# Graph network: every sixth group gathers three tiles, ScalarE copies the columns of the fourth

## The chip, the cores and the metric

The kernel runs on one core of a Trainium2 chip. The metric is the device time of one execution in microseconds; the time before is the median of three runs.

## The reference

Two message-passing layers over 6250 nodes with 128 features and 200,000 edges, which are sorted by destination. In each layer every edge takes a row of its source, a row of its destination and its own 128 features:

```python
# layer 0
m = relu(concat([x[dst], x[src], edge_attr, u[0]]) @ W1.T + b1)
x = layernorm(x + relu(concat([x, segment_sum(m, dst), u[0]]) @ W2.T + b2))
# layer 1
h = relu(concat([x[src], x[dst], edge_attr]) @ msg_w1 + msg_b1)
agg = segment_sum(h @ msg_w2 + msg_b2, dst) / counts
x = layernorm(x + relu(concat([x, agg]) @ upd_w1 + upd_b1) @ upd_w2 + upd_b2)
```

The product with the concatenation is a sum of three products, so what an edge needs of its source is one row of q = x @ wq (128 fp32 numbers), and of its destination one row of p = x @ wp + b.

## The kernel before

**Tiles.** Edges go in groups of 512 = 4 tiles (J = 4) of 128 (P); there are NG = 391 groups in a layer, numbered i = l * NG + g over both. The tables of q (tabQ, one for each layer) and p (tabP, three bf16 pieces to a row) lie in DRAM.

**One group.** GpSimd gathers the q rows of its edges into the ring Q, which holds R_Q = 10 groups: one indirect DMA a tile (L319), by the list of sources srcE in SBUF. The gather of group i waits until VectorE's addition of group i - 10 is done. TensorE multiplies the transposed edge features by wc into a PSUM bank (L1119, fp32) and adds the p rows with a one-hot matrix ST that VectorE makes (L1302, L1124). VectorE adds bank and Q into M (L1405), ScalarE applies the relu to M in place (L1287), and TensorE sums the edges of a destination with a second one-hot matrix S (L1392, L1137), two groups later in its order. VectorE adds these sums to AC (L1429) at a column that it reads from a register; registers come from baseI in SBUF (L960). ScalarE waits for the addition of each group before its relu, and TensorE for the relu.

**What runs beside it.** In layer 0, groups 2 to 40, the rest of tabP is made, a chunk every three groups (rows_product, rows_hi, rows_mid, rows_store). When all edges of a block of nodes ("unit" u, 14 of them) are summed, its update follows in steps that are spread over groups by the tables DUE and STEPS: first and second (normalisation), norm, x1t (transposition), xt_copy (to XT), q1, q_copy (store to tabQ and, for the early units, tabE), hi, mid, p_store. XT holds the transposed x: of layer 0 until a unit's update, of layer 1 from then on. Layer 1 gathers its first three groups (EARLY, 12 gathers) from tabE and then waits for the whole of tabQ. Each engine runs its own program in order; where an engine waits, all that stands behind it on that engine waits too. Before all this, 20 gathers fetch raw rows of x (L325), which are multiplied by wq on the chip.

Of the kernel before, what the change touches and what calls it, by code (L numbers as in the profile page):

```python
# [8 lines left out]
I32 = mybir.dt.int32  # L9
# [5 lines left out]
N = 6250  # L15
# [85 lines left out]


# [19 lines left out]
def build(nc, a, out):  # L122
    ctx = ExitStack()
    with ctx:
# [44 lines left out]
        srcR = sb("srcR", [P, RAW * J], I32)  # L169
        vsum = sb("vsum", [P, 1])  # L170
# [59 lines left out]
        p1 = {n: sem(f"p1_{n}") for n in ("c", "hi", "r", "mid", "lo")}  # L230
        s_mz, s_mean, s_ind, s_u, s_ru, s_meet = (sem(n) for n in ("s_mz", "s_mean", "s_ind", "s_u", "s_ru", "s_meet"))
# [76 lines left out]

        def q_count(i):
            return 16 * sum(tiles(x % NG) for x in range(i % R_Q, i + 1, R_Q))  # L310
# [96 lines left out]
        def start_scalar(e):  # L407
            e.dma_start(wall[:, 0:D], a["wall"][:, 0:D]).then_inc(s_wq, 16)
            for i in range(1, len(XG), 2):
                x_load(e, i)  # L410
            e.dma_start(wall[:, NLATE:NW], a["wall"][:, NLATE:NW]).then_inc(s_wl, 16)
            e.dma_start(rows3[:, :, :].rearrange("p a d -> p (a d)"), a["rows"].broadcast_to([3, 4 * D])).then_inc(s_row, 16)
            e.dma_start(baseI[:, :], a["base"]).then_inc(s_bas, 16)
            e.dma_start(basE, a["base"].broadcast_to([P, NGP])).then_inc(s_bas, 16)
            e.dma_start(cb[:, :], a["rows"][:, 3 * D:4 * D].broadcast_to([P, D])).then_inc(s_cb, 16)
            for c in range(1, NC, 2):
                n = CH[c][1]
                e.wait_ge(s_q, c + 1)
# [40 lines left out]
        def start_vector(e):  # L459
# [7 lines left out]
            def bases_to_rows():  # L467
                e.wait_ge(s_bas, 32)
# [152 lines left out]
        def general_gpsimd(e, l):  # L621
            q = gs[l]
            e.wait_ge(q["z"], 16)
            if l == 0:
                for r in range(PF):
                    e.wait_ge(f_q[r], 16 * J)
# [380 lines left out]
        def fast_tensor(e):  # L1007
# [31 lines left out]
            def q1(u):  # L1039
# [4 lines left out]
                for k in range(n):  # L1044
                    last = e.matmul(bank[o][:, k * D:(k + 1) * D], XT[:, (b + k) * P:(b + k + 1) * P], wq[1], start=(k == 0), stop=(k == n - 1))  # L1045
# [4 lines left out]
                for k in range(n):  # L1050
                    last = e.matmul(bank[3][:, k * D:(k + 1) * D], XT[:, (b + k) * P:(b + k + 1) * P], wp[1], start=False, stop=(k == n - 1))  # L1051
# [6 lines left out]
            def hidden(u):  # L1058
# [47 lines left out]
            for l in range(2):  # L1106
                for g in range(LAST + 6):
                    i = l * NG + g
                    if g < NG:
# [51 lines left out]
        def fast_scalar(e):  # L1161
# [90 lines left out]

            for l in range(2):
                for g in range(LAST + 11):
                    if l == 0:
# [27 lines left out]
                    if g < NG:  # L1283
                        i = l * NG + g
                        e.wait_ge(v_tt, i + 1)
                        m = M[:, i % R_M, 0:tiles(g), :].rearrange("p j d -> p (j d)")
                        e.activation(m, m, ACT.Relu).then_inc(v_rl, 1)  # L1287

        def fast_vector(e):
# [49 lines left out]
            def second(l, u):  # L1339
# [5 lines left out]
                if l == 0:  # L1345
                    e.memset(AC[:, 0, b * P:(b + n) * P], 0.0).then_inc(s_mz, 1)
# [30 lines left out]
            for l in range(2):  # L1377
                ctl = 2 - l
                for g in range(LAST + 10):
# [13 lines left out]
                    if 1 <= g < NG + 1:  # L1393
# [10 lines left out]
                        n = tiles(g - 1)  # L1404
# [12 lines left out]
                    if 3 <= g < NG + 3 and last_of(l * NG + g - 3):  # L1417
# [8 lines left out]
                        if w == NWIN:  # L1426
# [3 lines left out]
                                        ALU.add).then_inc(v_ag, 1)  # L1430
                    if l == 0:
# [131 lines left out]
def laid_out(v):  # L1563
    import numpy as _np

    def cut(m, b):
# [18 lines left out]
        "srcL": srcp.astype(_np.int32).reshape(NGP, J, P).transpose(2, 0, 1).reshape(P, NGP * J),  # L1585
        "dstL": dstp.astype(_np.int32).reshape(NGP, J, P).transpose(2, 0, 1).reshape(P, NGP * J),
# [23 lines left out]
```

## Time and profile before

| | us |
|---|---|
| runs, median (lowest to highest) | 3929.21 (3928.15 to 3929.58) |
| profiled execution, its span | 3929.8 |
| GpSimd busy | 2960.2 |
| TensorE matmul busy, weight loads busy | 3229.0, 2975.7 |
| VectorE busy | 1583.8 |
| ScalarE busy | 590.4 |

The profile is of one execution; beside its span it gives no other time of it. Busy time is that of the instructions an engine executes. Instructions that only its sequencer handles (registers, semaphores, issuing a DMA) are not counted. "Issue" is idle time in which the engine waited for nothing that the profile shows. PE stands for TensorE's matmuls, PEld for its weight loads, DVE for VectorE, ACT for ScalarE, POOL for GpSimd, SP for SyncE; a q behind a name is its sequencer. PEclk is the granted share of TensorE's full speed, 2.4 GHz.

### The profile page before, as it was taken

The numbers are of one execution on the slowest core, as the hardware profiler recorded it, in microseconds if no ns is written. First come the engines' busy times: TensorE is split into PE (matmuls) and PEld (weight loads), VectorE is DVE, ScalarE is ACT, GpSimd is POOL, SyncE is SP. The second block draws the span as 40 slices with busy tenths as digits, with TensorE's granted clock in tenths as the row PEclk, the third lists the DMA queues.
The fourth block names the chain that finished last, engine by engine and source line by source line (L and its number), as shares of the span: only waits on it lengthen the run. The fifth ranks groups of instructions, "written<-read, shape, count | busy, mean of one in ns | idle before, by whom it ended". The sixth has DMA issues, their size and how long they took to land.

```text
span 3929.8 us, 45222 instructions
## 1 busy us (share of the span) xinstructions
PE 3229.0 (82%) x16881; PEld 2975.7 (76%) x16881; DVE 1583.8 (40%) x3640; ACT 590.4 (15%) x1017; POOL 2960.2 (75%) x3156
## 2 busy tenths in 40 slices
PE   6988888888788888888878888878888888888887
PEld 6877777777777777777778777777777777777776
DVE  6533334343444444444543333333433333333333
ACT  1211111111111111111111111111111111111111
POOL 7777777777777777777777777777777777777776
PEclk7755555565655556665665555555555555555556
DMA  7644444444444444445454444444444444444443
GB/s 261 200 138 134 135 136 143 132 133 139 148 139 149 149 149 147 147 147 154 131 158 135 133 131 124 135 139 136 139 136 141 139 142 137 140 135 141 142 142 100
DMA packets 257760, 563.18 MB, mean 143 GB/s; under 512 B 131254, under 2 KB 151713, under 8 KB 232572
## 3 DMA queue, kind: packets, MB, share of 16 engines
q1 hardware_dynamic: 132824, 332.20, 25.4%
q0 software_dynamic: 100032, 205.00, 19.8%
q10 hardware_dynamic: 24676, 23.01, 1.7%
q8 instruction: 135, 2.21, 0.2%
q14 instruction: 93, 0.76, 0.1%
HBM read 537.29 MB, written 22.66 MB: 142 GB/s over the span
## 4 chain that ended last, share of the span: by engine, by line
POOL 70%; issue 23%; DMA 4%; DVE 2%; PE 2%; ACT 0%; SPq 0%; POOLq 0%; DVEq 0%
POOL Qr L319 70%; DMA Qr<-tabQ,srcE 3%; DVE BIG L1405 1%; PE bank L1137 0%; DMA srcE<-in_srcL 0%; DVE BIG L1302 0%; PE bank L1119 0%; PE bank L1092 0%; DVE BIG L1392 0%; DMA tabQ<-BIG 0%; DVE BIG L1400 0%; PE bank L1051 0%; PE bank L1045 0%; DVE AC L609 0%; POOL Qr L325 0%
## 5 line engine op out<-in xcount | busy, mean ns | idle before, releaser
L319 POOL DMA_INDIRECT Qr<-tabQ,srcE x3094 | 2925.3, 945 | 942.9 <-issue 933.2
L1137 PE MATMUL bank<-BIG 128*128 128x42 f32 x6252 | 1379.0, 396 | 143.6 <-ACT BIG L1287 141.1
L1119 PE MATMUL bank<-wall,BIG 128*128 128x128 f32 x6252 | 1473.0, 410 | 19.1 <-DMA BIG<-tabP 19.1
L1137 PEld LDWEIGHTS bank<-BIG 128*128 128x128 f32 x6252 | 1307.5, 308 | 207.6 <-ACT BIG L1287 201.5
L1302 DVE TENSOR_TENSOR BIG<-bank,BIG 126x512 bf16<-126x512 f32 x782 | 539.3, 690 | 2264.7 <-DMA Qr<-tabQ,srcE 2254.8
L1119 PEld LDWEIGHTS bank<-wall,BIG 128*128 128x128 f32 x6252 | 1311.5, 309 | 23.8 <-issue 23.8
L1287 ACT ACTIVATE BIG<-BIG 128x512 f32<-128x512 f32 (+1 forms) x782 | 492.1, 629 | 3229.1 <-DVE BIG L1405 3220.4
L1124 PE MATMUL bank<-BIG 126*128 126x128 bf16 x3126 | 490.2, 295 | 506.5 <-DVE BIG L1302 396.7
L1124 PEld LDWEIGHTS bank<-BIG 126*128 126x128 bf16 x3126 | 342.0, 135 | 639.0 <-DVE BIG L1302 455.9
L1405 DVE TENSOR_TENSOR BIG<-bank,Qr 128x512 f32<-128x512 f32 (+1 forms) x782 | 532.7, 681 | 41.2 <-PE bank L1124 25.3
L1392 DVE TENSOR_TENSOR BIG<-bank,relE 128x168 f32<-128x168 f32 x782 | 252.6, 323 | 3.5 <-DMA Qr<-tabQ,srcE 3.5
L1400 DVE TENSOR_REDUCE BIG<-BIG 128x42 bf16<-128x168 f32 (+2 forms) x263 | 151.7, 577 | 0.0
L1429 DVE TENSOR_TENSOR AC<-AC,bank 128x84 f32 (+1 forms) x526 | 111.1, 211 | 6.7 <-PE bank L1137 3.2
L1140 PEld LDWEIGHTS bank<-BIG,onesb 128*128 128x128 bf16 x263 | 70.4, 268 | 0.0
L1140 PE MATMUL bank<-BIG,onesb 128*128 128x42 bf16 x263 | 60.5, 230 | 0.0
L609 DVE RECIPROCAL AC<-AC 128x512 f32<-128x512 f32 (+1 forms) x13 | 41.1, 3159 | 0.0
L1013 PE MATMUL bank<-wall,XT 128*128 128x128 f32 x98 | 26.1, 444 | 0.0
L1013 PEld LDWEIGHTS bank<-wall,XT 128*128 128x128 f32 x98 | 21.9, 326 | 5.4 <-issue 5.2
L1056 PE MATMUL bank<-XT,wall 128*128 128x512 f32 (+2 forms) x28 | 25.4, 1019 | 0.0
L325 POOL DMA_INDIRECT Qr<-in_x,srcR x20 | 20.6, 1031 | 6.0 <-issue 5.7
L1045 PE MATMUL bank<-wall,XT 128*128 128x128 f32 x98 | 23.1, 404 | 0.9 <-ACT XT L1180 0.9
L1026 PE MATMUL bank<-wall,AC 128*128 128x128 f32 x98 | 23.0, 410 | 0.4 <-DVE AC L1429 0.4
(137 smaller groups left out, 609.9 us busy)
## 6 DMA issues: line engine op xcount, KB each, us to landing
BIG<-in_eaT SPq DMA_DIRECT2D x194, 1024.0 KB, 5.4
BIG<-in_dstR SPq DMA_DIRECT2D x194, 504.0 KB
Qr<-tabQ,srcE POOLq DMA_INDIRECT x3094
BIG<-tabP SPq DMA_DIRECT2D x526, 31.5 KB
tabP<-BIG ACTq DMA_DIRECT2D x22, 384.0 KB, 3.1
tabQ<-BIG ACTq DMA_DIRECT2D x17, 256.0 KB, 5.2
X<-in_xN SPq DMA_DIRECT2D x1, 3136.0 KB, 16.8
tabE<-BIG ACTq DMA_DIRECT2D x11, 256.0 KB, 2.3
```

Of the source, the lines that this page charges most:

```text
L319: e.indirect_dma_start(Q[0:p, i % R_Q, j, :], None, table[:, :], bass.IndirectOffsetOnAxis(ap=srcE[0:p, g, j:j + 1], axis=0)).then_inc(f_q ...
L1013: e.matmul(bank[o][:, k * D:(k + 1) * D], XT[:, (b + k) * P:(b + k + 1) * P], w2T[0], start=False, stop=False)
L1119: e.matmul(bank[i % R_C][:, j * D:(j + 1) * D], f_eaT[:, k % R_EA, (g % LQ * J + j) * P:(g % LQ * J + j + 1) * P], wc[l], start=(j == 0), ...
L1124: last = e.matmul(bank[i % R_C][:, j * D:(j + 1) * D], ST[0:K, i % R_ST, j * P:(j + 1) * P], PB[0:K, w % R_PB, :], start=False, stop=(j == ...
L1137: last = e.matmul(sums[:, 0:W], M[:, i % R_M, j, :], S[:, hot(i), j, :], start=(j == 0 and first_of(i)), stop=(j == n - 1 and last_of(i)))
L1140: last = e.matmul(sums[:, W:2 * W], onesb[:, :], S16[:, w % R_S, :], start=True, stop=True)
L1287: e.activation(m, m, ACT.Relu).then_inc(v_rl, 1)
L1302: e.tensor_tensor(ST[0:K, i % R_ST, :], bank[6][0:K, g:g + 1].broadcast_to([K, GE]), bc[0:K, k % R_BC, (g % LQ) * GE:(g % LQ + 1) * GE], A ...
L1392: e.tensor_tensor(S[:, hot(i), :, :], io, rel, ALU.is_equal).then_inc(v_s, 1)
L1400: e.tensor_reduce(S16[:, w % R_S, :], S[:, h:hot(i) + 1, :, :].rearrange("p r j w -> p w (r j)"), AX, ALU.add).then_inc(v_cn, 1)
L1405: e.tensor_tensor(M[:, i % R_M, 0:n, :].rearrange("p j d -> p (j d)"), bank[i % R_C][:, 0:n * D], Q[:, i % R_Q, 0:n, :].rearrange("p j d - ...
L1429: e.tensor_tensor(acc, acc, bank[4 + w % 2][:, 0:ctl * W].rearrange("p (t w) -> p t w", w=W), ALU.add).then_inc(v_ag, 1)
```

## The change

In groups 10, 16, 22, ... to 388 of layer 0 and from 16 on in layer 1, GpSimd gathers three tiles. The fourth tile's part of q is not gathered: ScalarE copies the columns of XT that belong to the tile's 128 sources into a tile XC (ring of two), and TensorE multiplies that by wq straight into the group's bank. The 128 columns are copied in six parts of 20, 20, 24, 20, 20 and 24, one behind each group's relu, in the six groups 6n to 6n + 5 for the tile of group 6n + 10. Each part loads its column numbers from colI (SBUF) into registers; each copy takes one column, 128 partitions by one element. VectorE adds only three tiles in such a group, and ScalarE takes the relu of the fourth from the bank. As XT must keep the x of layer 0 until the last such tile, xt_copy writes layer 1's x to AC, which is free by then; q1 reads it there; and xt_move copies it to XT at the end of layer 0, from group 384 on, the last three units in group 0 of layer 1, behind which VectorE clears AC.

```diff
+MOVES = [(0, NG - 7 + u // 2) for u in range(NU - 3)] + [(1, 0)] * 3
+MOVED = 2
+COPIERS = ((6, 10),)
+TAKEN = [[[n * per + lead for n in range(NG) if n * per + lead < NG - 2 and n * per >= (0, MOVED)[l]] for l in range(2)]
+         for per, lead in COPIERS]
...
+def col_piece(k, l, g):
+    per, lead = COPIERS[k]
+    n, q = divmod(g, per)
+    if n * per + lead not in TAKEN[k][l]:
+        return None
+    return col_tile(l * NG + n * per + lead)[1], COL_ROW[k] + n, 4 * (q * P // 4 // per), 4 * ((q + 1) * P // 4 // per), q == 0
...
+        def gathered(i):
+            return tiles(i % NG) - (col_tile(i) is not None)
...
-                for j in range(tiles(g)):
+                for j in range(gathered(i)):
                     p = VP if g == NG - 1 and j == VJ else P
                     e.indirect_dma_start(Q[0:p, i % R_Q, j, :], None, table[:, :],
...
-                    last = e.matmul(bank[o][:, k * D:(k + 1) * D], XT[:, (b + k) * P:(b + k + 1) * P], wq[1], start=(k == 0), stop=(k == n - 1))
+                    last = e.matmul(bank[o][:, k * D:(k + 1) * D], AC[:, 0, (b + k) * P:(b + k + 1) * P], wq[1], start=(k == 0), stop=(k == n - 1))
...
+                        if col_tile(i) is not None:
+                            h, c = col_tile(i)
+                            e.wait_ge(s_col[h], COPIERS[h][0] * (c + 1))
+                            e.matmul(bank[i % R_C][:, (J - 1) * D:J * D], XC[h][:, c % R_X, :], wq[l], start=False, stop=False)
...
-                e.copy(XT[:, b * P:(b + n) * P], bank[unit_bank(0, "x1t", u)][:, 0:n * P]).then_inc(u_tc, 1)
+                e.copy(AC[:, 0, b * P:(b + n) * P], bank[unit_bank(0, "x1t", u)][:, 0:n * P]).then_inc(u_tc, 1)
+
+            def xt_move(u):
+                b, n = UN[u]
+                e.wait_ge(u_tc, u + 1)
+                if u == 0:
+                    for k, (per, _) in enumerate(COPIERS):
+                        e.wait_ge(s_col[k], per * len(TAKEN[k][0]))
+                e.copy(XT[:, b * P:(b + n) * P], AC[:, 0, b * P:(b + n) * P]).then_inc(s_mv, 1)
...
+            def columns(l, g):
+                if col_piece(0, l, g) is None:
+                    return
+                c, row, lo, hi, new = col_piece(0, l, g)
+                if new and c >= R_X:
+                    e.wait_ge(v_C, col_group(0, c - R_X) + 1)
+                if new and c == len(TAKEN[0][0]):
+                    e.wait_ge(s_mv, NU)
+                _, at = nc.values_load_multi_w_load_instructions(
+                    colI[row:row + 1, lo:hi], engines=[mybir.EngineType.Activation], min_val=0, max_val=N - 1,
+                    skip_runtime_bounds_check_because="the source of an edge, which is a node")
+                for x in range(lo, hi):
+                    last = e.copy(XC[0][:, c % R_X, x:x + 1], XT[:, bass.ds(at[x - lo], 1)])
+                last.then_inc(s_col[0], 1)
...
-                        m = M[:, i % R_M, 0:tiles(g), :].rearrange("p j d -> p (j d)")
-                        e.activation(m, m, ACT.Relu).then_inc(v_rl, 1)
+                        m = M[:, i % R_M, 0:gathered(i), :].rearrange("p j d -> p (j d)")
+                        last = e.activation(m, m, ACT.Relu)
+                        if col_tile(i) is not None:
+                            last = e.activation(M[:, i % R_M, J - 1, :], bank[i % R_C][:, (J - 1) * D:J * D], ACT.Relu)
+                        last.then_inc(v_rl, 1)
+                        columns(l, g)
...
-                if l == 0:
-                    e.memset(AC[:, 0, b * P:(b + n) * P], 0.0).then_inc(s_mz, 1)
+
+            def clear(u):
+                b, n = UN[u]
+                e.wait_ge(s_mv, u + 1)
+                e.memset(AC[:, 0, b * P:(b + n) * P], 0.0).then_inc(s_mz, 1)
```

The order of the instructions shows it in three places. GpSimd's whole list of gathers, before:

```order
L325 DMA Qr<-in_x,srcR 128x128 x20
L319 DMA Qr<-tabQ,srcE 128x128 x20
L1454 TENSOR_LOAD flagI
L1454 ISA x2
L1491 COMPARE_AND_BRANCH
L319 DMA Qr<-tabQ,srcE 128x128 x1522
L319 DMA Qr<-tabQ,srcE 64x128
L319 DMA Qr<-tabE,srcE 128x128 x12
L319 DMA Qr<-tabQ,srcE 128x128 x1550
L319 DMA Qr<-tabQ,srcE 64x128
```

and now:

```order
L361 DMA Qr<-in_x,srcR 128x128 x20
L355 DMA Qr<-tabQ,srcE 128x128 x20
L1533 TENSOR_LOAD flagI
L1533 ISA x2
L1570 COMPARE_AND_BRANCH
L355 DMA Qr<-tabQ,srcE 128x128 x1458
L355 DMA Qr<-tabQ,srcE 64x128
L355 DMA Qr<-tabE,srcE 128x128 x12
L355 DMA Qr<-tabQ,srcE 128x128 x1487
L355 DMA Qr<-tabQ,srcE 64x128
```

Of the two long runs on tabQ, 64 gathers left the first and 63 the second; all else stands as it stood.

ScalarE around group 10 of layer 0, before (L1287 is the relu of a group, L1251 the store of a chunk of tabP, L1243 and L1247 its two copies):

```order
L1243 CAST BIG<-bank 128x4x128
L1287 ACTIVATE BIG<-BIG 128x512
L1251 DMA tabP<-BIG 128x4x384
L1287 ACTIVATE BIG<-BIG 128x512
L1247 CAST BIG<-bank 128x4x128
L1287 ACTIVATE BIG<-BIG 128x512
```

and now, in group 10 (L1356 and L1358 are the relus, L1312 the register load, L1316 the pairs of a register instruction, ISA, and a copy of one column):

```order
L1302 DMA tabP<-BIG 128x4x384
L1356 ACTIVATE BIG<-BIG 128x384
L1358 ACTIVATE BIG<-bank 128x128
L1312 TENSOR_LOAD colI
L1316 ISA
L1316 COPY XC<-XT 128x1
L1316 ISA
```

The relu has become two, and a load and 20 or 24 pairs stand between it and the next group's relu; before there was nothing between most relus.

TensorE around group 10, before (L1119 the edge features, L1124 the p rows, L1137 the sums, L1140 the counts):

```order
L1119 MATMUL bank<-wall,BIG 128x128 x4
L1124 MATMUL bank<-BIG 128x128 x4
L1137 MATMUL bank<-BIG 128x42 x4
L1140 MATMUL bank<-BIG,onesb 128x42
L1119 MATMUL bank<-wall,BIG 128x128 x4
L1124 MATMUL bank<-BIG 128x128 x4
L1137 MATMUL bank<-BIG 128x42 x4
```

and now:

```order
L1158 MATMUL bank<-wall,BIG 128x128 x4
L1167 MATMUL bank<-BIG 128x128 x4
L1180 MATMUL bank<-BIG 128x42 x4
L1183 MATMUL bank<-BIG,onesb 128x42
L1158 MATMUL bank<-wall,BIG 128x128 x4
L1162 MATMUL bank<-wall,XC 128x128
L1167 MATMUL bank<-BIG 128x128 x4
L1180 MATMUL bank<-BIG 128x42 x4
```

One product with XC (L1162) was put in between the edge features and the p rows of that group.

## Rows read from the trace of the kernel before

**Rows 1.** Head and part 1 of the page: busy us (share) xinstructions.

```profile
span 3929.8 us, 45222 instructions
...
PE 3229.0 (82%) x16881; PEld 2975.7 (76%) x16881; DVE 1583.8 (40%) x3640; ACT 590.4 (15%) x1017; POOL 2960.2 (75%) x3156
```

**Rows 2.** The chain that ended last, part 4 of the page, by engine.

```profile
POOL 70%; issue 23%; DMA 4%; DVE 2%; PE 2%; ACT 0%; SPq 0%; POOLq 0%; DVEq 0%
```

**Rows 3.** The waits: who waited for whom, us in total, times, longest.

```profile
POOL Qr L319 <- issue: 936.9, 3074, 0.3
...
PEld bank L1119 <- issue: 23.8, 15, 9.7
...
POOL Qr L319 <- DVE BIG L1405: 9.8, 32, 0.3
```

**Rows 4.** The timeline of GpSimd around 3000 us: start, duration, idle before.

```profile
2999.45 0.94 POOL L319 DMA_INDIRECT Qr<-tabQ,srcE  x1 [0.30 <-issue]
...
3001.95 0.94 POOL L319 DMA_INDIRECT Qr<-tabQ,srcE  x1 [0.30 <-issue]
```

**Rows 5.** GpSimd on tile Qr: duration min/median/max, first and last start.

```profile
L319 POOL DMA_INDIRECT Qr<-tabQ,srcE x3094: 899/944/2462, 30.5 to 3912.6; - x194
L325 POOL DMA_INDIRECT Qr<-in_x,srcR x20: 940/944/1710, 3.8 to 29.2; - x20
L319 POOL DMA_INDIRECT Qr<-tabE,srcE x12: 940/944/957, 1958.5 to 1972.2; - x12
```

**Rows 6.** Groups of ScalarE with forms apart: count, busy us, mean ns, idle before.

```profile
L1287 ACT ACTIVATE BIG<-BIG 128x512 f32<-128x512 f32 x780 | 491.0, 630 | 3225.3 <-DVE BIG L1405 3216.6 <-issue 7.8 <-ACT BIG L1174 0.9
...
L1165 ACT ACTIVATE BIG<-BIG 128x1 f32<-128x1 f32 x2 | 0.4, 203 | 1.4 <-DVE BIG L1337 1.4
```

**Rows 7.** Windows of the start and of layer 1.

```profile
core 0: us, PE busy (x) PEld busy (x) DVE busy (x) ACT busy (x) POOL busy (x), PEclk, DMA share, GB/s
83.00:145.00 62.00, 59.89 (x440) 56.29 (x441) 41.05 (x77) 17.49 (x30) 46.76 (x51) 0.80 0.64 199
2000.00:2500.00 500.00, 410.54 (x2048) 385.39 (x2047) 180.65 (x345) 63.46 (x101) 378.40 (x400) 0.52 0.45 137
```

**Rows 8.** Register loads of L960, a stretch with one each and one with four.

```profile
L960 SPq TENSOR_LOAD <-baseI x26: 523/533/602, 2004.1 to 2494.8; - x26
L960 DVEq TENSOR_LOAD <-baseI x25: 302/306/313, 2012.4 to 2491.2; - x25
...
L960 DVEq TENSOR_LOAD <-baseI x63: 339/342/364, 2602.9 to 3840.0; - x63
```

**Rows 9.** The timeline of ScalarE at the end of layer 0.

```profile
1962.67 0.20 ACT L1165 ACTIVATE BIG<-BIG 128x2 f32<-128x2 f32 x1 [1.83 <-DVE BIG L1337]
1962.78 0.35 ACT L1209 CAST BIG<-bank 128x256 bf16<-128x256 f32 x1
...
1970.46 0.33 ACTq L1195 DMA_DIRECT2D tabQ<-BIG  x1
```

**Rows 10.** L1429, one register instruction and the addressed instruction behind it.

```profile
L1429 DVEq FUSED_REGOPS  x1: 46/46/46, 65.3 to 65.3; - x1
L1429 DVE TENSOR_TENSOR AC<-AC,bank x1: 242/242/242, 65.4 to 65.4; 128x84 f32 x1
```

**Rows 11.** Two timelines of VectorE: four tiny instructions, and two.

```profile
612.87 0.38 DVE L1335 BATCH_NORM_AGGREGATE BIG<-BIG 128x2 f32<-128x6 f32 x4
...
1962.19 0.25 DVE L1335 BATCH_NORM_AGGREGATE BIG<-BIG 128x2 f32<-128x6 f32 x2
```

**Rows 12.** Timelines of VectorE and GpSimd at the start: first addition, eleventh group.

```profile
52.90 0.69 DVE L1405 TENSOR_TENSOR BIG<-bank,Qr 128x512 f32<-128x512 f32 x1 [2.21 <-PE bank L1124]
...
57.10 0.94 POOL L319 DMA_INDIRECT Qr<-tabQ,srcE  x1 [0.30 <-issue]
```

More of the change, by code:

```diff
@@ L100, with col_tile, col_group @@
 LAST = BASE[-1]
+MOVES = [(0, NG - 7 + u // 2) for u in range(NU - 3)] + [(1, 0)] * 3
[3 more added lines that the diff above has]
+         for per, lead in COPIERS]
+COL_ROW = [sum(len(TAKEN[x][0]) for x in range(k)) for k in range(len(COPIERS))]
+COL_ROWS = [i for t in TAKEN for i in t[0]]
+R_X = 2
+def col_tile(i):
+    l, g = divmod(i, NG)
+    for k in range(len(COPIERS)):
+        if l < 2 and g in TAKEN[k][l]:
+            return k, len(TAKEN[k][0]) * l + TAKEN[k][l].index(g)
+    return None
+def col_group(k, c):
+    return TAKEN[k][0][c] if c < len(TAKEN[k][0]) else NG + TAKEN[k][1][c - len(TAKEN[k][0])]
+def col_piece(k, l, g):
+    per, lead = COPIERS[k]
+    n, q = divmod(g, per)
+    if n * per + lead not in TAKEN[k][l]:
+        return None
+    return col_tile(l * NG + n * per + lead)[1], COL_ROW[k] + n, 4 * (q * P // 4 // per), 4 * ((q + 1) * P // 4 // per), q == 0
 ROWS = [2 + SPACED * (c - UPFRONT) for c in range(NC)]
@@ L169, in build @@
         srcR = sb("srcR", [P, RAW * J], I32)
+        colI = sb("colI", [P, P], I32)
+        XC = [sb(f"XC{k}", [P, R_X, P]) for k in range(len(COPIERS))]
         vsum = sb("vsum", [P, 1])
@@ L230, in build @@
         p1 = {n: sem(f"p1_{n}") for n in ("c", "hi", "r", "mid", "lo")}
+        s_col = [gs[1]["bt"], gs[1]["ct"]]
+        s_mv = gs[1]["bv"]
         s_mz, s_mean, s_ind, s_u, s_ru, s_meet = (sem(n) for n in ("s_mz", "s_mean", "s_ind", "s_u", "s_ru", "s_meet"))
@@ L307, in tiles @@
             return -(-VALID // P) if g == NG - 1 else J
+        def gathered(i):
+            return tiles(i % NG) - (col_tile(i) is not None)
         def q_count(i):
-            return 16 * sum(tiles(x % NG) for x in range(i % R_Q, i + 1, R_Q))
+            return 16 * sum(gathered(x) for x in range(i % R_Q, i + 1, R_Q))
         def gathers(e, l, g0, g1, table):
@@ L414, in start_scalar @@
             e.dma_start(basE, a["base"].broadcast_to([P, NGP])).then_inc(s_bas, 16)
+            e.dma_start(colI[0:len(COL_ROWS), :], a["srcC"]).then_inc(s_bas, 16)
             e.dma_start(cb[:, :], a["rows"][:, 3 * D:4 * D].broadcast_to([P, D])).then_inc(s_cb, 16)
@@ L428, in start_scalar @@
                 raw_copy(e, r)
+            e.wait_ge(s_bas, 48)
             e.wait_ge(s_wl, 16)
@@ L467, in bases_to_rows @@
             def bases_to_rows():
-                e.wait_ge(s_bas, 32)
+                e.wait_ge(s_bas, 48)
                 link(e.tensor_reduce(wrow[:, :], third[:, :], AX, ALU.add))
@@ L625, in general_gpsimd @@
                 for r in range(PF):
-                    e.wait_ge(f_q[r], 16 * J)
+                    e.wait_ge(f_q[r], 16 * gathered(r))
             e.sem_inc(q["done"], 1)
@@ L1050, in q1 @@
                 for k in range(n):
-                    last = e.matmul(bank[3][:, k * D:(k + 1) * D], XT[:, (b + k) * P:(b + k + 1) * P], wp[1], start=False, stop=(k == n - 1))
+                    last = e.matmul(bank[3][:, k * D:(k + 1) * D], AC[:, 0, (b + k) * P:(b + k + 1) * P], wp[1], start=False, stop=(k == n - 1))
                 last.then_inc(p_c, 1)
@@ L1251, in rows_store @@
                 e.dma_start(node_rows(tabP[0], c), fP3[:, c % R_U, 0:CH[c][1], :]).then_inc(s_tabP[0][c % R_PT], 16)
+            def columns(l, g):
[5 more added lines that the diff above has]
+                if new and c == len(TAKEN[0][0]):
+                    e.wait_ge(s_mv, NU)
+                _, at = nc.values_load_multi_w_load_instructions(
[4 more added lines that the diff above has]
+                last.then_inc(s_col[0], 1)
             for l in range(2):
                 for g in range(LAST + 11):
+                    for u in range(NU):
+                        if MOVES[u] == (l, g):
+                            xt_move(u)
                     if l == 0:
@@ L1403, in fast_vector @@
                             e.wait_ge(f_q[i % R_Q], q_count(i))
-                        n = tiles(g - 1)
+                        n = gathered(i)
                         e.tensor_tensor(M[:, i % R_M, 0:n, :].rearrange("p j d -> p (j d)"), bank[i % R_C][:, 0:n * D],
@@ L1430, in fast_vector @@
                                         ALU.add).then_inc(v_ag, 1)
+                    for u in range(NU):
+                        if MOVES[u] == (l, g):
+                            clear(u)
                     if l == 0:
@@ L1585, in laid_out @@
         "srcL": srcp.astype(_np.int32).reshape(NGP, J, P).transpose(2, 0, 1).reshape(P, NGP * J),
+        "srcC": srcp.astype(_np.int32).reshape(NGP, J, P)[COL_ROWS, J - 1],
         "dstL": dstp.astype(_np.int32).reshape(NGP, J, P).transpose(2, 0, 1).reshape(P, NGP * J),
```

## The prediction

> **What bounds the kernel now.** I read the page from its head down. The span is 3929.8 us; GpSimd is busy for 2960 us of it, ScalarE for 590 [rows 1]. The chain that ended last is GpSimd at 70% and "issue" at 23% [rows 2]. Both belong to the gather on L319: the table of waits gives its idle time to "issue", 3074 times and never over 0.3 us, and the 32 waits for VectorE are no longer than that either [rows 3]. So GpSimd issues gathers back to back, one in 1.249 us (2999.45 and 3001.95 are two apart), of which 0.945 is busy and 0.30 issue, whatever the other engines do [rows 4]. There are 20 + 3094 + 12 = 3126 of them, the first at 3.8 us and the last at 3912.6 [rows 5], and 3126 x 1.249 = 3904 us: the span but for its two ends. A group of four tiles costs 4.99 us, and everything else must fit in that.
>
> ScalarE spends (590.4 - 491.0)/782 = 0.13 us a group beside its relu of 0.63 us, so it idles for over 4 us of each group [rows 1, 6]. TensorE is busy for 411 us in 500, 4.11 us a group, in a stretch where 0.52 of full speed was granted, mostly the lower level of 1.2 GHz [rows 7].
>
> **What the change removes.** Groups 10, 16, ..., 388 of layer 0 (64) and 16, 22, ..., 388 of layer 1 (63): 127 gathers, as the order has it (1522 to 1458, 1550 to 1487). 127 x 1.249 = **158.6 us**, as long as GpSimd stays the engine that nobody holds up. The mean group then lasts 2999 x 1.249 / 782 = 4.79 us. Were only the busy 0.945 us saved it would be 120 us, but every gather has its 0.30 of issue, so I count that too.
>
> **What it adds on ScalarE.** Nearly every group gets one register load and 20 or 24 pairs of a register instruction and a copy of one column, on average 127 x 128 / 782 = 20.8. No row of before has this, so I bound it.
>
> The load: VectorE's takes 0.306 us where one register is loaded and 0.342 where four are, 0.012 for each further one; SyncE's with one takes 0.533 [rows 8]. With 20 to 24 registers that is 0.54 to 0.81 us; I take 0.7.
>
> A pair, from below: the data path alone. A small square root of 0.20 us starts at 1962.67 and the next instruction at 1962.78 [rows 9], so it holds the engine for 0.11 us; a column copy cannot hold it much longer. From above: nothing overlaps, 0.203 us for a 128x1 instruction [rows 6] and 0.046 for the register instruction ahead of it [rows 10], 0.25 us. Between the two stands the sequencer, which has to pass on both. From the start of a register instruction to that of the addressed instruction behind it are 0.1 us, 65.3 to 65.4 [rows 10]. Four tiny instructions take 0.38 us where two take 0.25 [rows 11], so one is passed on in 0.07 us or less. 0.046 + 0.07 = 0.12 us if the two follow each other on the sequencer, 0.1 + 0.07 = 0.17 us if the copy has reached the data path before the next is begun. I take **0.13 us a pair**, near the lower, since the 0.1 holds the way to the data path, which need not keep the sequencer: 2.7 us a group.
>
> Laid end to end, ScalarE's group is 0.13 + 0.63 + 0.7 + 2.7 = 4.2 us, under 4.79, hidden behind the gathers with 0.6 us to spare. That cover is gone at a pair of (4.79 - 1.46)/20.8 = **0.16 us**; I keep 0.11 and 0.25 us for the rivals. The forecast hangs on this narrow step.
>
> The Trainium skill, in "ScalarE: Activation LUTs" (What ACT_TABLE_LOAD costs), gives an instruction without pointer operands 186 ns and 0.833 per element and says that neighbours overlap by about 93 ns; by it a column copy holds the data path for 94 ns, and the estimate stays at 158.6 us saved. The same skill, in "VectorE: DVE Perf Modes" (The TRN2 errata), charges a ScalarE instruction from SBUF 224 cycles plus its elements at 1.2 GHz, 187.5 ns for one column. That speaks against this change: with it ScalarE would pace the kernel at 5.4 us a group, an estimate of 4270 us in all. The trace's 0.11 us from start to start is with the first.
>
> **Instruction supply.** ScalarE goes to some 33,000 instructions. TensorE runs 16,881 matmuls and as many weight loads already [rows 1], and its largest wait for "issue" sums to 23.8 us [rows 3]. I cost it at nothing.
>
> **TensorE.** 127 products of 128x128 in fp32, two matmul instructions each. The mean of all its instructions is 3229.0 / 16881 = 0.19 us [rows 1], so a product is 0.4 us, or 0.8 were each twice the mean: 0.07 to 0.13 us per group, and 4.11 + 0.13 = 4.2 us is under 4.79. It waits for columns whose copies ended five groups earlier, so that wait should be empty. The taken tile's relu is one more small ScalarE instruction, under 0.6 us once in six groups: at most 0.1. VectorE's addition gets shorter. Nothing of it is on the path.
>
> **The ends of the layers.** x of layer 1 passes through AC and is copied to XT from group 384 on, two copies of at most 0.63 us a group, when the columns of the layer are done (group 383). The last three units are moved and cleared in group 0 of layer 1. The chain there is tight: the last store of tabQ is issued at 1970.46 [rows 9], and the first gather that reads it follows the last one of tabE, at 1972.2 + 1.25 [rows 5], 3 us later. The moves stand behind these stores on ScalarE and VectorE's memsets leave the step ahead of them, so I add nothing; were the store later than its slack, GpSimd would lose just the excess.
>
> **The start.** From group 2 to 40 ScalarE also has two copies and a DMA every three groups, some 0.5 us a group: 4.2 + 0.5 = 4.7 us, almost the 4.79. The ring of Q holds ten groups: the first addition starts at 52.90, and the gather that needs it at 57.10, 3.5 us after its end [rows 12]. TensorE is busy for 59.89 of 62 us in this stage [rows 7]. I take **2 us** of waiting, between 0 and 12.
>
> **Sum.** Against the profiled execution's 3929.8 us, 0.6 over the median of the timed runs: 3929.8 - 158.6 + 2 = 3773.2; from the median 3772.6. **3773 us.** The runs shown agree within 1.5 us; 0.2%, 8 us, is what I count as no change.
>
> **Rivals.**
> (a) *GpSimd goes on pacing*, as summed: 3766 to 3780. Chance 0.74.
> (b) *The ring runs dry in stretches*: ScalarE keeps up in the mean, but not in groups 0 to 42, where rows of P are made beside the columns, or behind the change of layers. At 5.4 us a group for 42 groups it loses 0.6 x 42 = 25 us: 3798. For it: the spare 0.6 us is used up there. Against: GpSimd was not held up at all in this stage although TensorE was full. 3780 to 3830, chance 0.10.
> (c) *ScalarE becomes the pace*, since the sequencer's two steps and the data path do not overlap. The time is 70 us (the 53 ahead of the first addition and 17 behind the last gather) + 782 x (1.46 + 20.8 c). At c = 0.20 us, 5.62 us a group: 4465 us. At 0.25: 5280 us. From c = 0.167 on it is slower than before. For it: nothing in before runs 20 such pairs in a row, and 0.17 was my upper end for the sequencer. Against: the neighbours in rows 9 overlap. Chance 0.12. The second rule of the skill above is this rival.
> (d) *The two nearly cancel*: c from 0.158 to 0.167, between 3780 and 3930 us, mostly a smaller gain. Chance 0.03. The last 0.01 is a gather whose own pitch changes.
>
> **Numbers.** (a) and (b) hold 0.84, so the range goes from 3766 (no waiting, and 5 for scatter) to 3830. Faster: 0.74 + 0.10 + 0.03 = 0.87; same: 0.01; slower: 0.12.
>
> **What would show it.** Right: the gather's line with 2967 instructions and 1.249 us from one to the next, no wait over 0.3 us but at the start; ScalarE with 16,256 column copies, one in 0.13 us or less, and idle before its relu because of VectorE's addition. Wrong: gathers that wait for VectorE's addition, that for TensorE, TensorE for the relu, and ScalarE without idle time. Then a pair costs over 0.16 us, and the forecast fails by that single term.

## The result and the profile after

The changed kernel takes 3775.45 us (median of 4 runs, 3774.86 to 3777.05), the one before 3929.39 (4 runs): ratio 0.9608, 95% interval 0.9595 to 0.9622. The profiled execution took 3777.05 us, its span is 3775.3. The forecast was 3773 us in a range from 3766 to 3830.

Head and parts 1, 3 and 4 of the page of the changed kernel (beside [rows 1, 2]):

```profile
span 3775.3 us, 79022 instructions
...
PE 3100.1 (82%) x17135; PEld 2877.4 (76%) x17135; DVE 1564.4 (41%) x3640; ACT 2165.4 (57%) x17414; POOL 2836.8 (75%) x3029
...
q14 instruction: 353, 2.89, 0.2%
...
POOL 67%; issue 23%; DMA 5%; DVE 3%; PE 2%; ACT 1%; ACTq 0%; SPq 0%; POOLq 0%; DVEq 0%
```

GpSimd and "issue" still make up 90% of the chain. ScalarE went from 15% to 57% busy and has 1% of the chain; that is what a filled, but covered, engine looks like.

GpSimd on tile Qr (beside [rows 5]):

```profile
L355 POOL DMA_INDIRECT Qr<-tabQ,srcE x2967: 903/944/2433, 30.0 to 3758.1; - x198
L361 POOL DMA_INDIRECT Qr<-in_x,srcR x20: 940/944/1307, 3.8 to 28.8; - x20
L355 POOL DMA_INDIRECT Qr<-tabE,srcE x12: 940/944/951, 1883.4 to 1897.2; - x12
```

These are 2999 gathers where 3126 stood, at the same duration of 944 ns. The waits (beside [rows 3]):

```profile
POOL Qr L355 <- issue: 898.2, 2940, 2.5
ACT BIG L1356 <- DVE BIG L1481: 879.8, 312, 17.2
ACT XC L1316 <- issue: 649.0, 990, 2.1
...
POOL Qr L355 <- DVE BIG L1481: 17.3, 39, 5.7
```

The second row is ScalarE's spare time: 880 us before its relu, in 312 waits, or 1.1 us for each of 782 groups on the mean. The third is new: ScalarE's data path stands idle before a column copy for what the profile calls issue. Nearly all of it is the register load: the timelines below have 0.71 us idle for a load of 20 registers and 1.03 for one of 24, which makes some 620 us over 762 loads. The last row shows one wait of 5.7 us that before had not (0.3 at most): here GpSimd was held up.

The new instructions, by the lines of the register load and of the copy:

```profile
L1312 ACTq TENSOR_LOAD <-colI x762: 1242/1297/2832, 53.2 to 3732.3; - x191
...
L1316 ACTq FUSED_REGOPS  x16256: 37/37/43, 54.5 to 3736.0; - x199
L1316 ACT COPY XC<-XT x16256: 174/187/193, 54.6 to 3736.1; 128x1 f32 x199
```

ScalarE's timeline in layer 1, and the register load that lies in it (its line, from 2401.5 on):

```profile
2401.63 0.56 ACT L1316 COPY XC<-XT 128x1 f32 x5 [0.16 <-issue]
2402.10 0.62 ACT L1356 ACTIVATE BIG<-BIG 128x512 f32<-128x512 f32 x1
2403.44 1.95 ACT L1316 COPY XC<-XT 128x1 f32 x20 [0.71 <-issue]
2405.29 0.52 ACT L1356 ACTIVATE BIG<-BIG 128x384 f32<-128x384 f32 x1
2405.72 0.25 ACT L1358 ACTIVATE BIG<-bank 128x128 f32<-128x128 f32 x1
```

```profile
L1312 ACTq TENSOR_LOAD <-colI x1: 1292/1292/1292, 2402.0 to 2402.0; - x1
```

Twenty copies take 1.95 us, of which the last lasts 0.187: (1.95 - 0.187)/19 = 0.093 us from one to the next, although each is listed with 187 ns. The load of 20 registers takes 1.29 us, one of 24 that starts at 1853.2 takes 1.54. It starts when the last copy is passed on, so the relu (2402.10 to 2402.72) runs under it. From relu to relu are 3.19 us, not the 4.2 of the forecast.

Windows of the start and of layer 1 (beside [rows 7], the same columns):

```profile
83.00:145.00 62.00, 53.24 (x414) 49.95 (x413) 35.86 (x67) 47.23 (x369) 47.05 (x50) 0.86 0.63 187
2000.00:2500.00 500.00, 419.05 (x2130) 393.07 (x2129) 188.69 (x379) 281.82 (x2335) 378.09 (x401) 0.54 0.43 138
```

TensorE is busy for 419.05 of 500 us: with a group of 4.79 us that is 4.01 us a group, where it was 410.54 x 4.996 / 500 = 4.10 (the prediction has 4.11). GpSimd issues 401 gathers in 500 us, where it issued 400.

**Where the time went.** From gather to gather I summed what exceeds 1.249 us, over all gaps beyond 1.30. At the start (first 60 gathers) it is 3.0 us, before 3.4; around the change of layers 7.8, before 0.5; in the rest of layer 1 0.9, before 3.9. So 3929.8 - 158.6 - 0.4 + 7.3 - 3.0 = 3775.1, and the span is 3775.3. The forecast had a wait of 2 us at the start in place of the -0.4, and neither the 7.3 us nor the 3.0; the 7.3 are the largest part that it missed. Timelines of VectorE, ScalarE and GpSimd there:

```profile
1858.09 1.03 DVE L1422 MEMSET AC<- 128x512 f32 x2 [4.73 <-ACT XT L1231]
...
1862.78 1.02 DVE L1422 MEMSET AC<- 128x512 f32 x2 [1.20 <-ACT XT L1231]
...
1854.90 2.32 ACT L1316 COPY XC<-XT 128x1 f32 x24 [1.03 <-issue]
1857.31 1.14 ACT L1231 COPY XT<-AC 128x512 f32<-128x512 f32 x2
...
1880.92 0.33 ACTq L1245 DMA_DIRECT2D tabE<-BIG  x1
...
1876.81 0.90 POOL L355 DMA_INDIRECT Qr<-tabQ,srcE  x1 [0.30 <-issue]
1883.43 0.95 POOL L355 DMA_INDIRECT Qr<-tabE,srcE  x1 [5.72 <-DVE BIG L1481]
...
1900.59 0.94 POOL L355 DMA_INDIRECT Qr<-tabQ,srcE  x1 [2.48 <-issue]
```

Read from the top: VectorE's first clearing of AC is queued ahead of the next group's one-hot matrix and addition, and it waits 4.73 us for the move on ScalarE (L1231), which stands behind the last 24 copies. Each later group has a clearing with a wait of some 1.2 us and 1.0 us of memset. VectorE's programme is late from there on, the last store of tabE is issued only at 1880.92, and GpSimd's first gather from it starts 5.72 us after the end of the one ahead; the first from tabQ has 2.48 us.

### The profile page after: what moved, and what is told of

It reads as the page before. It is cut to its first block, busy times and chain, and to the rows that moved or that the text cites. A ratio compares the mean times of both kernels' runs of the same rounds, so it can differ in the third digit from the quotient of the medians.

```text
span 3775.3 us, 79022 instructions
## 1 busy us (share of the span) xinstructions
PE 3100.1 (82%) x17135; PEld 2877.4 (76%) x17135; DVE 1564.4 (41%) x3640; ACT 2165.4 (57%) x17414; POOL 2836.8 (75%) x3029
## 3 DMA queue, kind: packets, MB, share of 16 engines
q14 instruction: 353, 2.89, 0.2%
## 4 chain that ended last, share of the span: by engine, by line
POOL 67%; issue 23%; DMA 5%; DVE 3%; PE 2%; ACT 1%; ACTq 0%; SPq 0%; POOLq 0%; DVEq 0%
POOL Qr L355 67%; DMA Qr<-tabQ,srcE 4%; DVE BIG L1481 1%; PE bank L1158 1%; PE bank L1180 1%; DMA BIG<-tabP 0%; ACT XC L1316 0%; DVE BIG L1375 0%; DVE BIG L1476 0%; DMA srcE<-in_srcL 0%; DVE BIG L1468 0%; ACT BIG L1356 0%; ACTq L1312 0%; PE bank L1167 0%; PE bank L1051 0%
## 5 line engine op out<-in xcount | busy, mean ns | idle before, releaser
L355 POOL DMA_INDIRECT Qr<-tabQ,srcE x2967 | 2802.4, 945 | 906.5 <-issue 894.9
L1316 ACT COPY XC<-XT 128x1 f32 x16256 | 1605.2, 187 | 655.2 <-issue 649.0
L1180 PE MATMUL bank<-BIG 128*128 128x42 f32 x6252 | 1307.0, 381 | 198.6 <-ACT BIG L1356 165.2
L1180 PEld LDWEIGHTS bank<-BIG 128*128 128x128 f32 x6252 | 1238.6, 294 | 260.1 <-ACT BIG L1356 215.4
L1158 PE MATMUL bank<-wall,BIG 128*128 128x128 f32 x6252 | 1395.8, 394 | 15.8 <-DMA BIG<-tabP 15.8
L1158 PEld LDWEIGHTS bank<-wall,BIG 128*128 128x128 f32 x6252 | 1239.1, 293 | 20.2 <-issue 20.1
L1356 ACT ACTIVATE BIG<-BIG 128x512 f32<-128x512 f32 (+1 forms) x782 | 476.6, 609 | 887.2 <-DVE BIG L1481 879.8
L1167 PE MATMUL bank<-BIG 126*128 126x128 bf16 x3126 | 470.1, 289 | 375.3 <-DVE BIG L1375 286.1
L1162 PE MATMUL bank<-wall,XC 128*128 128x128 f32 x254 | 75.4, 397 | 0.0
L1162 PEld LDWEIGHTS bank<-wall,XC 128*128 128x128 f32 x254 | 64.4, 310 | 0.0
L1121 PE MATMUL bank<-wall,BIG 128*128 128x128 f32 x98 | 21.9, 389 | 14.7 <-ACT BIG L1273 14.7
L1358 ACT ACTIVATE BIG<-bank 128x128 f32<-128x128 f32 x127 | 32.4, 255 | 0.0
```

The source lines that it names most:

```text
L1162: e.matmul(bank[i % R_C][:, (J - 1) * D:J * D], XC[h][:, c % R_X, :], wq[l], start=False, stop=False)
L1167: last = e.matmul(bank[i % R_C][:, j * D:(j + 1) * D], ST[0:K, i % R_ST, j * P:(j + 1) * P], PB[0:K, w % R_PB, :], start=False, stop=(j == ...
L1180: last = e.matmul(sums[:, 0:W], M[:, i % R_M, j, :], S[:, hot(i), j, :], start=(j == 0 and first_of(i)), stop=(j == n - 1 and last_of(i)))
L1316: last = e.copy(XC[0][:, c % R_X, x:x + 1], XT[:, bass.ds(at[x - lo], 1)])
L1356: last = e.activation(m, m, ACT.Relu)
```

## The experiments

**The ScalarE side alone.** All gathers, VectorE's whole addition and the old relu stay; the copies and the moves are there, the product of the copied columns isn't.

```diff
-            return tiles(i % NG) - (col_tile(i) is not None)
+            return tiles(i % NG)
...
-                            e.matmul(bank[i % R_C][:, (J - 1) * D:J * D], XC[h][:, c % R_X, :], wq[l], start=False, stop=False)
...
-                        if col_tile(i) is not None:
-                            last = e.activation(M[:, i % R_M, J - 1, :], bank[i % R_C][:, (J - 1) * D:J * D], ACT.Relu)
```

> All ScalarE work, moves and clears of the change stay, but GpSimd gathers all four tiles again; the product with XC and the separate relu are left out, so the copied columns are not used. If the gathers alone set the time and ScalarE is hidden: 3926 to 3938 us, the time of before, with no more than a few us for the moves. If the saving came from something else than the 127 gathers (VectorE's shorter addition, the other order at the layer change): near 3775 us.

Measured: 3932.93 us (10 runs, 3931.51 to 3934.61) against 3929.94, ratio 1.0007 (0.9998 to 1.0017). Waits and the gather's line:

```profile
ACT BIG L1355 <- DVE BIG L1478: 1017.4, 400, 17.1
POOL Qr L355 <- issue: 937.2, 3071, 1.5
```

```profile
L355 POOL DMA_INDIRECT Qr<-tabQ,srcE x3094: 903/944/2452, 30.0 to 3915.3; - x194
```

The 16,256 copies cost nothing that the timed runs can tell while they are covered, and the gain goes with the 127 gathers. The 3 us more are within the interval; in the trace the gaps around the change of layers sum to 4.4 us, where before had 0.5.

**One block copy in place of the single copies.** Columns lo to hi are copied at once, with no load and no register instruction; they are the wrong columns.

```diff
-                _, at = nc.values_load_multi_w_load_instructions(
-                    colI[row:row + 1, lo:hi], engines=[mybir.EngineType.Activation], min_val=0, max_val=N - 1,
...
-                for x in range(lo, hi):
-                    last = e.copy(XC[0][:, c % R_X, x:x + 1], XT[:, bass.ds(at[x - lo], 1)])
+                last = e.copy(XC[0][:, c % R_X, lo:hi], XT[:, lo:hi])
```

> ScalarE makes one copy of 20 or 24 fixed neighbouring columns instead of a register load and 20 or 24 single copies, so XC holds wrong columns; 127 gathers fewer as in the change. If ScalarE's 16,256 copies are hidden but for the layer change: 3768 to 3775 us, and what is won comes from the wait of the first clear there. If ScalarE costs nothing anywhere: 3775 within 2 us. If ScalarE holds the ring up elsewhere too, below 3768 us is not possible either, as 2999 gathers at 1.249 us and the two ends need 3766.

Measured: 3772.53 us (3771.99 to 3772.87), ratio 0.9598 (0.9582 to 0.9614). ScalarE's idle time before its relu is 2979.6 us here and 879.8 in the changed kernel:

```profile
ACT BIG L1352 <- DVE BIG L1477: 2979.6, 768, 16.3
```

So 2100 us of ScalarE's time, 2.7 us a group, are taken up by loads and single copies, and the kernel's time is within the intervals the same without them. What little differs lies at the change of layers, where the gaps between gathers sum to 2.9 us instead of 7.8. That is still 2.4 more than before.

**Half as many copies more, and twice as many.** Further copies into an unused half of a wider XC, from the registers already computed.

```diff
-                for x in range(lo, hi):
-                    last = e.copy(XC[0][:, c % R_X, x:x + 1], XT[:, bass.ds(at[x - lo], 1)])
+                for x in [*range(P + lo, P + hi, 2), *range(lo, hi)]:
+                    last = e.copy(XC[0][:, c % R_X, x:x + 1], XT[:, bass.ds(at[x % P - lo], 1)])
```

The second kernel has a step of 1 in place of 2.

> The change with 1.5 times the single copies: every second column is copied once more to a spare half of XC, which nobody reads. It tells how ScalarE's parts add up. If the relu hides under the register load (0.13 + 1.35 load + 31.2 x 0.0925 = 4.4 us a group, under the 4.79 of the gathers): 3775 to 3790 us. If relu, load and copies lie end to end, as the prediction laid them (0.13 + 0.63 + 1.35 + 2.89 = 5.0 us): 70 + 782 x 5.0 = 3980 us.

> The change with twice the single copies, the second set to a spare half of XC. With the relu under the load ScalarE needs 0.13 + 1.35 + 41.6 x 0.0925 = 5.33 us a group, over the 4.79 of the gathers: 70 + 782 x 5.33 = 4240 us, slower than before the change. If all lie end to end (5.96 us): 4730 us. If the sequencer and the data path need only what the gathers leave free, 3775 us.

Measured: 3776.92 us (3775.84 to 3777.89), ratio 0.9611 (0.9595 to 0.9627), with half more; 3859.55 us (3854.19 to 3864.96), ratio 0.9816 (0.9799 to 0.9832), with twice as many. The first tells against laying relu, load and copies end to end. The second is a miss of mine, 4240 expected. ScalarE's timeline with twice as many, and the load in it:

```profile
2403.86 4.54 ACT L1316 COPY XC<-XT 128x1 f32 x48
2408.31 0.62 ACT L1356 ACTIVATE BIG<-BIG 128x512 f32<-128x512 f32 x1
2408.84 3.27 ACT L1316 COPY XC<-XT 128x1 f32 x32
```

```profile
L1312 ACTq TENSOR_LOAD <-colI x2: 1263/1386/1510, 2402.2 to 2407.4; - x2
L1316 ACTq FUSED_REGOPS  x16256: 37/37/43, 54.8 to 3824.4; - x199
```

There is no gap between relu and copies. There are 32,512 copies but still 16,256 register instructions: for the second half of a run the sequencer has only copies to pass on, gets ahead of the data path, and starts the load at 2407.4, a microsecond before the data path is through with the copies. The data path takes (4.54 - 0.187)/47 = 0.093 us a copy with or without a register instruction ahead. So a load costs ScalarE time only when nothing is queued in front of it, as in the changed kernel, where each copy has its register instruction and the sequencer is never ahead. This is read from the trace; no run varied it by itself, but the idle time put down to issue before the copies goes with it: 649 us in the changed kernel, 292 with half more copies and 101 with twice as many. ScalarE is 93% busy here and has 56% of the chain, GpSimd 13%: it is just too slow, and GpSimd's waits have one of 48.8 us at the change of layers (below).

**AC cleared two groups later.** The clearing stands behind two more groups in VectorE's programme, nothing else moves.

```diff
+CLEARS = [(l, g + 2 * (l == 0)) for l, g in MOVES]
...
-                        if MOVES[u] == (l, g):
+                        if CLEARS[u] == (l, g):
                             clear(u)
```

> The change with VectorE's clears of AC two groups after ScalarE's moves instead of in the same group; nothing else. In the changed kernel the first clear waited 4.7 us for ScalarE and each later one 1.2 us, and GpSimd then stood for 5.4 us before the first gather of tabE and for 2.2 us before that of tabQ. If the clears' waits are the cause of the loss at the layer change: 3768 to 3772 us and those gaps gone or under 1 us each. If it is ScalarE, whose moves and stores stand behind its columns: 3774 to 3777 us.

**Moves earlier.** The moves begin in group 378 (one a group), the clearings follow one group later, and the last copied tile of layer 0 is left to its gather.

```diff
-MOVES = [(0, NG - 7 + u // 2) for u in range(NU - 3)] + [(1, 0)] * 3
+MOVES = [(0, NG - 13 + u) for u in range(NU - 3)] + [(1, 0)] * 3
+CLEARS = [(l, g + 1 * (l == 0)) for l, g in MOVES]
...
-TAKEN = [[[n * per + lead for n in range(NG) if n * per + lead < NG - 2 and n * per >= (0, MOVED)[l]] for l in range(2)]
+TAKEN = [[[n * per + lead for n in range(NG) if n * per + lead < (NG - 8, NG - 2)[l] and n * per >= (0, MOVED)[l]] for l in range(2)]
```

> Layer 0 takes no tile after group 382, so the columns end at group 377; one move a group from 378 on, each clear one group later. One gather more (126 fewer than before, not 127), 1.25 us. If the two moves and two clears a group delay the update of the last units: 3768 to 3772 us with no gap at the layer change. If the gaps come from something else, 3776 to 3778 us.

Measured: 3772.99 us (5 runs, 3772.07 to 3774.63), ratio 0.9598 (0.9585 to 0.9611), with late clearings; 3773.52 (3772.71 to 3774.95), ratio 0.9598 (0.9585 to 0.9612), with early moves and one gather more. GpSimd's waits, first of the one, then of the other:

```profile
POOL Qr L356 <- DVE BIG L1482: 14.6, 48, 0.3
```

```profile
POOL Qr L356 <- DVE BIG L1482: 11.9, 39, 0.3
```

The wait of 5.7 us is gone in both: the gaps around the change of layers sum to 2.2 and 0.2 us instead of 7.8. That shows where the 7.3 us came from: 5.6 of them go with the place of the clearings alone. Of the 1.7 that are left the late clearings show one gap of 1.5 us before the first gather from tabE; it is gone where the moves are early too. In the timed ratios, 0.001 lower than the changed kernel's, it lies within the intervals.

**A copied tile in every fifth and in every fourth group,** each with the cure above (the moves begin in group 380, one a group, the clearings follow one group later, and layer 0 takes no tile after group 383). The parts are of 24 or 28 columns, and of 32.

```diff
-COPIERS = ((6, 10),)
+COPIERS = ((5, 8),)
```

The second kernel has ((4, 6),).

> The same with one tile in five groups (parts of 24 or 28 columns, 152 gathers fewer than before), moves one a group from 380 on. Per group ScalarE has 0.13 + 0.6 + 25.6 x 0.0925 = 3.1 us on its data path, and 4.1 us with a load of 1.6 us that does not overlap, against 4.75 us for the gathers. If the gathers go on pacing: 3929.9 - 152 x 1.249 = 3740 us, and up to 3 more. If ScalarE's load and copies lie end to end and with the node updates pass 4.75: above 3760 us.

> The same with one tile in four groups (32 columns a group, 190 gathers fewer), against 4.69 us of gathers a group. If the register load hides behind queued copies, as the run with twice the copies suggests, ScalarE has 0.13 + 0.6 + 32 x 0.0925 = 3.7 us: 3929.9 - 190 x 1.249 = 3693 us, and up to 15 more for the stretches with updates. If a load of 2.0 us and 2.96 us of copies lie end to end, 5.1 us a group: 70 + 782 x 5.1 = 4060 us.

Measured: 3741.19 us (5 runs, 3740.13 to 3741.86), ratio 0.9516 (0.9503 to 0.9529), with every fifth: faster than both kernels. 4144.48 us (4142.27 to 4151.52), ratio 1.0548 (1.0533 to 1.0562), with every fourth: slower than before. Of its expectation the dear case (4060 us) came true, and 84 us more. Waits, load and ScalarE's timeline with every fourth:

```profile
ACT XC L1317 <- issue: 1106.8, 1096, 2.7
...
POOL Qr L356 <- DVE BIG L1482: 493.5, 259, 28.2
...
PE bank L1163 <- ACT XC L1317: 139.7, 160, 2.7
```

```profile
L1313 ACTq TENSOR_LOAD <-colI x760: 1940/2013/3450, 54.0 to 4111.1; - x190
```

```profile
2401.45 0.62 ACT L1357 ACTIVATE BIG<-BIG 128x512 f32<-128x512 f32 x1
2403.47 3.06 ACT L1317 COPY XC<-XT 128x1 f32 x32 [1.40 <-issue]
2406.44 0.52 ACT L1357 ACTIVATE BIG<-BIG 128x384 f32<-128x384 f32 x1
```

This is what a ScalarE that paces looks like: no idle time before the relu, and before the copies only the rest of the load that the relu does not fill (1.40 us). From relu to relu are 2.02 + 2.97 = 4.99 us, where the gathers would need only 2936 x 1.249 / 782 = 4.69. GpSimd waits for the addition, and TensorE's product (L1163) for the columns. The last gather starts at 4092.7 us and the span ends 48 us later, in the changed kernel 17: that is 31 of the 84 us. The rest I did not take apart.

**Every fourth, the registers loaded once.**

```diff
-                _, at = nc.values_load_multi_w_load_instructions(
+                if not held:
+                    held.extend(nc.values_load_multi_w_load_instructions(
...
+                at = held
```

> The kernel with a copied tile in every fourth group, but its registers are loaded once, ahead of the first copy, and every later copy uses those 32 source numbers; so the columns copied are the wrong ones for all other groups, while the copies and the register instructions ahead of them stay 32 a group. In that kernel ScalarE's group was about 0.13 us of relu on the path, 2.01 us of load and 3.06 us of copies, 5.2 us in all. If the load is what makes it too long, a group here is 0.13 + 3.06 = 3.2 to 3.7 us, ScalarE has room again and GpSimd's transfers pace: 2936 x 1.249 + 26 to 40 us, so 3693 to 3710. If it is the copies themselves, or VectorE and TensorE under their load, the time stays near 4144, at least above 4000.

This expectation is wrong in one point: the register instructions do not stay. The addresses are computed once with the loaded registers, and the trace has 32 register instructions in all, so this kernel is without 759 of the 760 loads and without 24,288 of the 24,320 register instructions:

```profile
L1321 ACT COPY XC<-XT x24320: 173/187/217, 55.5 to 3652.2; 128x1 f32 x200
L1321 ACTq FUSED_REGOPS  x32: 37/37/43, 55.4 to 58.6; - x32
```

**The changed kernel, each load done twice.**

```diff
-                _, at = nc.values_load_multi_w_load_instructions(
-                    colI[row:row + 1, lo:hi], engines=[mybir.EngineType.Activation], min_val=0, max_val=N - 1,
-                    skip_runtime_bounds_check_because="the source of an edge, which is a node")
+                two = [nc.values_load_multi_w_load_instructions(
+                    colI[row:row + 1, lo:hi], engines=[mybir.EngineType.Activation], min_val=0, max_val=N - 1,
+                    skip_runtime_bounds_check_because="the source of an edge, which is a node")[1] for _ in range(2)]
+                at = [two[k % 2][k] for k in range(hi - lo)]
```

> The changed kernel with each piece's registers loaded twice (even columns use the first load's, odd columns the second's); everything else is the same. If each load holds ScalarE's queue for its full 1.29 us (20 registers) or 1.53 us (24), a group is 0.13 + 2.58 + 1.95 = 4.7 us or 0.13 + 3.06 + 2.32 = 5.5 us, 4.9 on the mean of four and two, over the 4.79 us that GpSimd's transfers give: 782 x 4.9 + 70 = 3900 us, at least above 3850. If a second load right behind the first is mostly hidden (it was 0.7 us or less, as the prediction took the first), a group stays under 4.4 us and the time is that of the changed kernel, 3773 to 3780.

Measured: 3691.58 us (4 runs, 3690.99 to 3692.26), ratio 0.9393 (0.9377 to 0.9408), with one load; 3967.0 us (4 runs, 3961.98 to 3971.77), ratio 1.0090 (1.0074 to 1.0107), with double loads. ScalarE's timelines in this order:

```profile
2400.07 3.05 ACT L1321 COPY XC<-XT 128x1 f32 x32
2404.05 0.52 ACT L1361 ACTIVATE BIG<-BIG 128x384 f32<-128x384 f32 x1 [0.94 <-DVE BIG L1486]
```

```profile
2403.72 0.62 ACT L1357 ACTIVATE BIG<-BIG 128x512 f32<-128x512 f32 x1
2406.80 1.21 ACT L1317 COPY XC<-XT 128x1 f32 x12 [2.45 <-issue]
2408.17 1.21 ACT L1317 COPY XC<-XT 128x1 f32 x12 [0.17 <-issue]
2409.29 0.62 ACT L1357 ACTIVATE BIG<-BIG 128x512 f32<-128x512 f32 x1
```

With as many copies as the kernel that took 4144 us, but no loads, ScalarE waits 0.94 us before its relu and GpSimd paces again. By itself this kernel does not tell a load from the register instructions, which left with it; but a copy takes 0.093 us with or without one. The double loads change nothing but the loads: the copies start 3.08 us after the start of the relu, twice 1.54, and a kernel with 2999 gathers is 0.9% slower than the one with 3126. It is 67 us over the 3900 expected; the last gather starts at 3910.5, 59 us before the end of the span, where the changed kernel has 17, and that is 42 of them. The copies take more of a group than the load does (32 x 0.093 = 2.97 us beside the 1.40 that the data path stands idle), but what tips ScalarE over GpSimd's pace is the load.

## Why the prediction was right

- *GpSimd paces, 127 x 1.249 = 158.6 us saved* (rival (a), 0.74): right. The gathers keep their distance, and the issue behind them goes with them; with all gathers kept nothing is gained.
- *The pair of a register instruction and a copy, 0.13 us*: 0.093, by 0.04 us too dear, 0.8 us a group. Both bounds were above it: 0.11 was read from a root of two columns. In the trace the next register instruction starts within 0.01 us of the copy ahead of it: sequencer and data path work side by side, so that neither sum (0.12, 0.17) applied.
- *The load, 0.7 us, bounds 0.54 to 0.81*: 1.29 us for 20 registers, 1.54 for 24, outside the bounds. That is the step that failed. VectorE's rows, one and four registers, gave 0.012 us for each further one [rows 8]; on ScalarE it is (1.54 - 1.29)/4 = 0.06, and 2.01 us for 32 agree. The doubt was put on the copy alone ("the forecast fails by that single term"), while the load decides how far the change can be carried: rival (c) came true in the kernel with double loads and in the one with every fourth group, both times with c = 0.093. Here the forecast was saved by the room that was left, not by the term.
- *End to end 4.2 us*: the relu lies under the load. 0.13 + 1.37 (four loads of 1.29 and two of 1.54) + 20.8 x 0.093 = 3.4 us. Of three errors (pair -0.8, load +0.7, relu -0.6) two cancel; that the sum was safe was partly luck.
- *TensorE, 0.07 to 0.13 us a group more*: the product's matmuls last 397 ns in the page's rows and are busy for 75.4 us, 0.10 us a group, hidden as said. That the busy time per group still fell, from 4.11 to 4.01, goes with a granted clock of 0.54 instead of 0.52 there.
- *Instruction supply, nothing*: right for the time, but not free. ScalarE loses 0.26 us in each of 242 breaks (last section), 64 us in all or 0.08 us a group, and it is covered.
- *The start, 2 us*: 0.4 us less waiting than before (3.0 for 3.4). At 3.4 + 0.5 us a group nothing ran dry (rival (b)).
- *The ends of the layers, nothing*: 7.3 us. I named the 3 us of slack and VectorE's memsets, but not that a clearing waits for a move that waits for the copies, with the additions of the last groups queued behind it. The late clearings and the early moves confirm it. It is also where a sign of being right failed: no gather was to wait over 0.3 us but at the start, and two waited for 5.72 and 2.48.
- The two misses in the sum, -2.4 and +7.3, and less scatter in layer 1 (-3.0) leave 3775.1 for the span beside 3773.2. That they nearly cancel is luck.

The Trainium skill, "ScalarE: Activation LUTs" (What ACT_TABLE_LOAD costs), gives an ACTIVATE without pointer operands 186 ns and 0.833 per element and lets neighbours overlap by about 93; for one column that is an estimate of 94 ns. The 0.093 us measured from start to start in runs of copies agrees. The same skill, "VectorE: DVE Perf Modes" (The TRN2 errata), charges 224 cycles plus the elements at 1.2 GHz, an estimate of 187.5 ns for one column. The trace's *duration* of a copy is just that, 187 ns, but a run of them is paced by half of it, so the 4270 us did not come.

## What to carry over

When work is put on an engine that idles, price what its sequencer does by itself (register loads above all, by their number of registers) apart from what its data path does, and see what is queued when the sequencer stops: the same load was free behind copies already passed on, and without them it kept the copies back for 1.3 us, of which the relu filled 0.6. Carry such a change in steps and watch the idle time before the engine's own critical instruction, 1.1 us a group with every sixth, 0.5 (378.8 / 782) with every fifth and 0.1 (52.5 / 782) with every fourth, which was already slower than before. Look at the seams apart: one wait placed ahead of others' work cost more than 16,256 covered copies.

## What the runs showed of the hardware that was not expected

- A register load on ScalarE grows by 0.06 us a register (1.29 us at 20, 1.54 at 24, 2.01 at 32); on VectorE it was 0.012 from one to four. The loads of the kernel with every fifth group, of 24 and 28 registers, lie in between:

```profile
L1313 ACTq TENSOR_LOAD <-colI x760: 1472/1545/3267, 53.6 to 3699.9; - x190
```

- Where ScalarE paces, its lag first eats up the ring of Q, in which the gathers may be ten groups ahead, and little of it shows as waiting; at a seam it comes due at once. With twice the copies GpSimd waits 48.83 us before its first gather from tabE, about ten groups of 4.79 us, and 48.9 us with double loads. The same is seen at the end of the kernel, where 28 us (twice the copies) and 59 us (double loads) lie behind the start of the last gather, and 17 in the changed kernel. That the length of the ring sets these numbers is my reading; no run changed the ring:

```profile
1911.46 0.90 POOL L355 DMA_INDIRECT Qr<-tabQ,srcE  x1 [0.30 <-issue]
1961.19 0.96 POOL L355 DMA_INDIRECT Qr<-tabE,srcE  x1 [48.83 <-DVE BIG L1481]
```

- Runs of copies are broken by gaps of mostly 0.15 to 0.17 us "issue". In the changed kernel 242 neighbouring copies start 0.34 to 0.39 us apart instead of 0.093. In ScalarE's list of instructions, the sequencer's included, nearly all of these places lie 127 to 129 instructions apart, or twice that, and the instruction queue moved 2.89 MB in 353 packets, 8.2 KB each, instead of 0.76 MB in 93. That points to the supply of instructions, a block of 128 at a time; it is an inference from these counts, and no run varied it. TensorE was not held up more by it: its largest wait for "issue" sums to 20.1 us, before 23.8. In the kernel with one load, where the copies have no register instructions ahead of them, a single such gap is left in 24,320 copies.
